# Gate and up of six shared chunks of batches 0 and 1 made jointly, in seven block products

## What is computed

```python
# layer 0: mixture of experts; each expert and the shared one is a gated MLP, 256 -> 1024 -> 256
mlp = lambda x, g, u, d: (gelu(x @ g) * (x @ u)) @ d
x = x + mlp(x, shared) + sum(w[b, e] * mlp(x, skill[e]) for the top 2 experts e of softmax(cond_8[b]))
# layer 1: one expert (argmax of cond_8[b]), 256 -> 512 -> 256, with biases
x = x + (silu(x @ Wu.T + bu) * (x @ Wg.T + bg)) @ Wd.T + bd
# layer 2: x + x @ (sum_g cond_8[b, g] * weight[g] * mask).T + bias
# layer 3: x + x @ W_base.T + b_base + 2 * sum_e cond_8[b, e] * (x @ A[e].T) @ B[e].T
```

## Time and profile before

| | |
|---|---|
| median of 3 runs | 483.42 us (483.36 to 483.56) |
| span of the profiled execution, from its first to its last instruction | 481.8 us |
| its own time | not in the page; 1.6 us lie between its span and the runs' median |
| granted TensorE clock | 1.00 of full speed in all 40 slices |
| TensorE matmul | busy 477.8 us (99%), 2184 matmuls |
| TensorE weight load | 398.5 us (83%) |
| VectorE | 374.9 us (78%) |
| ScalarE | 262.7 us (55%) |
| DMA | 48.9 MB, mean 101 GB/s |

### The profile page before, as it was taken

How to read it: one execution, slowest core, us unless ns; L and a number is a source line. 1 busy time by engine, 2 the same in 40 slices (tenths; PEclk the granted TensorE clock), 3 DMA queues, 4 the chain that set the end, 5 groups by cost and what they waited for, 6 DMA issues and landing times.

```text
span 481.8 us, 6729 instructions
## 1 busy us (share of the span) xinstructions
PE 477.8 (99%) x2184; PEld 398.5 (83%) x2184; DVE 374.9 (78%) x642; ACT 262.7 (55%) x418; POOL 33.7 (7%) x56
## 2 busy tenths in 40 slices
PE   9999999999999999999999999999999999999997
PEld 7888888888888888888888888888888888888886
DVE  7678989969536578985988988998887799965465
ACT  5556555545446344555547566676765365544432
POOL 1910302000100200000000020000000100000000
PEclk9999999999999999999999999999999999999999
DMA  7988985386230532424290053404059224000002
GB/s 224 199 184 201 261 168 153 71 195 134 70 106 0 136 106 67 131 67 131 78 180 4 2 149 93 131 1 131 0 117 205 74 66 128 4 1 0 2 0 87
DMA packets 114538, 48.90 MB, mean 101 GB/s; under 512 B 66552, under 2 KB 113272, under 8 KB 114504
## 3 DMA queue, kind: packets, MB, share of 16 engines
q1 hardware_dynamic: 111360, 42.88, 35.9%
q0 software_dynamic: 2560, 5.21, 4.5%
q10 hardware_dynamic: 584, 0.39, 0.3%
HBM read 46.36 MB, written 2.10 MB: 101 GB/s over the span
## 4 chain that ended last, share of the span: by engine, by line
PE 99%; DVE 0%; DVEq 0%; issue 0%
PE bank_a L1568 9%; PE bank_a L1569 9%; PE bank_b L1569 9%; PE bank_a L1570 9%; PE bank_b L1570 9%; PE bank_b L1568 9%; PE out L1593 6%; PE out L1596 6%; PE out L1592 6%; PE tail L1593 2%; PE tail L1596 2%; PE tail L1592 2%; PE tail L1570 2%; PE tail L1569 2%; PE tail L1568 2%; PE bank_a L1825 2%
## 5 line engine op out<-in xcount | busy, mean ns | idle before, releaser
L706 ACT ACTIVATE hid_hi<-hid 128x512 fp32r<-128x512 f32 x96 | 60.7, 632 | 93.2 <-DVE hid L968 54.0
L976 DVE TENSOR_TENSOR hid_lo<-hid,hid_hi 128x512 fp32r<-128x512 f32 x96 | 66.0, 687 | 16.8 <-ACT hid_hi L706 16.8
L698 ACT ACTIVATE hid<-bank_a 128x512 f32<-128x512 f32 x80 | 47.7, 596 | 55.1 <-PE bank_a L1570 54.3
L968 DVE SCALAR_TENSOR_TENSOR hid<-bank_b,mine,hid 128x512 f32<-128x512 f32 x64 | 47.7, 746 | 32.8 <-PE bank_b L1570 30.6
L956 DVE TENSOR_TENSOR w_lo<-raw,w_hi 128x768 fp32r<-128x768 f32 x57 | 54.1, 949 | 0.4 <-ACT w_hi L665 0.4
L1568 PE MATMUL bank_a<-x_hi,w_hi 128*128 128x512 f32 x114 | 44.5, 391 | 0.0
L1569 PE MATMUL bank_a<-x_lo,w_hi 128*128 128x512 f32 x114 | 44.5, 390 | 0.0
L1570 PE MATMUL bank_a<-x_hi,w_lo 128*128 128x512 f32 x114 | 44.4, 390 | 0.0
L1570 PE MATMUL bank_b<-x_hi,w_lo 128*128 128x512 f32 x114 | 44.4, 389 | 0.0
L1569 PE MATMUL bank_b<-x_lo,w_hi 128*128 128x512 f32 x114 | 44.4, 389 | 0.0
L1568 PE MATMUL bank_b<-x_hi,w_hi 128*128 128x512 f32 x114 | 44.4, 389 | 0.0
(11 more groups left out here) (346 smaller groups left out, 1108.9 us busy)
## 6 DMA issues: line engine op xcount, KB each, us to landing
raw<-in_L_cond_skill_gate SPq DMA_DIRECT2D x32, 256.0 KB, 3.0
raw<-in_L_cond_skill_up SPq DMA_DIRECT2D x32, 256.0 KB, 3.2
raw<-in_L_cond_skill_down SPq DMA_DIRECT2D x64, 128.0 KB, 3.3
raw<-in_L_cond_shared_down SPq DMA_DIRECT2D x22, 128.0 KB, 3.8
raw<-in_L_cond_shared_gate SPq DMA_DIRECT2D x10, 256.0 KB, 3.6
raw<-in_L_cond_shared_up SPq DMA_DIRECT2D x10, 256.0 KB, 3.7
raw_gate<-in_L_cond_W_gate SPq DMA_DIRECT2D x16, 128.0 KB, 3.0
early<-in_L_cond_weight POOLq DMA_DIRECT2D x2, 1024.0 KB, 7.6
```

The lines of the kernel that those rows point to most:

```text
L698: nc.scalar.activation(hid[:, tile_of(g)], bank_a[tile_of(g)][:, :], func, **kw).then_inc(act_ready, 1)
L706: nc.scalar.activation(hid_hi[:, tile_of(g)], hid[:, tile_of(g)], ACT.Copy).then_inc(hid_hi_ready, 1)
L968: ins = nc.vector.scalar_tensor_tensor(tile, bank, weight, tile, ALU.mult, ALU.mult)
L976: nc.vector.tensor_tensor(hid_lo[:, tile], hid[:, tile], hid_hi[:, tile].bitcast(F32), ALU.subtract).then_inc(hid_lo_ready, 1)
```

## The change

Batch 0 now has 2 shared chunks of its own (0, 1) and 16 expert chunks; batch 1 likewise. The other 6 shared chunks are made in 6 units for both, interleaved with chunks 12 to 17 of batch 0. So batch 0 is `first_head` (12 chunks) and 6 units, batch 1 is `second` (18 chunks with layers 1 to 3 of batch 0). The second pair keeps its 8 units. `pair_unit` and what it calls get the pair's first batch as an argument.

Constants (those that matter):

```diff
-MINE_AT = 3
-X_TURN_AT = {4: 1, 7: 2, 9: 3}
-L3_TURN_AT = 6
-L1_AFTER = 5
-C_AT = 13
-CA_AT = CH - 1
+PAIRED = {0: 0, 2: 6}
+JOINT = 2
+SHARED = 2
+OWN = (SHARED + 2 * MLP_CHUNKS, SHARED + 2 * MLP_CHUNKS, 2 * MLP_CHUNKS, 2 * MLP_CHUNKS)
+L1_PLACE = {1: 4, 2: 3, 3: OWN[3]}
+MINE_AT = 1
+X1_TURN_AT, X1_HI_AT, X1_LO_AT = 3, 4, 4
+W2_AT = 8
+T_AT = {5: 0, 7: 1, 9: 2, 10: 3}
+T_HI_AT = {8: ((0, 2), (2, 3)), 9: ((1, 4), (3, 5))}
+MAIN_AT = 10
+SUMS_AT = {0: 10, 2: 4}
+SUMS_LO_AT = {0: 11, 2: 5}
+C_PLACE = {0: 9, 1: 11, 2: 1, 3: 3}
+CA_PLACE = {6: 0, 14: 1}
+PAIR_TURN = {0: {1: 0, 2: 1, 3: 2, 4: 3}, 2: {1: 0, 2: 1, 4: 2, 6: 3}}
+PAIR_TURN_AT = {0: {2: 0, 3: 1, 4: 2, 5: 3}, 2: {2: 0, 3: 1, 5: 2, 7: 3}}
+PIECE_ORDER = ([("own", 0, c) for c in range(0, 14, 2)] + [("joint", 0, 2), ("own", 0, 14), ("joint", 0, 4), ("own", 0, 16), ("joint", 0, 6)]
+               + [("own", 1, c) for c in range(0, OWN[1], 2)]
```

SyncE's order. Piece 0 holds the two shared chunks of batch 0; every later piece is in the loop:

```diff
-            load_piece(1, None, *shared)
-            load_piece(2, None, *shared)
-            load_piece(3, splits_done(0, 1), *shared)
-            load_x(1)
             sp.wait_ge(chosen_ready, 1)
-            expert_pieces(0, 0, {1: lambda: load_x(2), 2: lambda: load_x(3)})
+            for j, (kind, b, c) in enumerate(PIECE_ORDER):
+                if j == 0:
+                    continue
...
+                load_piece(j, *(rows if kind == "own" and own_skill >= 0 else shared))
+                if (kind, b, c) == ("own", 0, 4):
+                    load_x(1)
+                if (kind, b, c) == ("own", 0, 14):
+                    for n in range(3):
+                        first_l1(n)
+                if (kind, b, c) == ("own", 1, 2):
+                    sp.wait_ge(turn_f, 3 * C1)
+                    load_x(2)
+                    load_x(3)
```

GpSimd's queue:

```diff
-            pool.wait_ge(x_turn, B - 1)
+            pool.wait_ge(x_turn, 1)
+            pool.wait_ge(split_lo, splits_done(0, W2_AT))
```

VectorE, at the start and in the new head of batch 0 (ScalarE casts the main weights of unit 0 in chunk `MAIN_AT`):

```diff
             first_parts(0)
+            take_chosen()
             first_x_parts(0)
...
+            take_picks()
+            first_head()
+            for m in range(UNITS[0]):
+                pair_unit(0, m)
+            second()
...
+            def first_head():
+                for i in range(UNIT_AT[0]):
...
+                    if i + SPLIT_AHEAD <= UNIT_AT[0]:
+                        split(0, i + SPLIT_AHEAD)
+                    if i:
+                        hidden_lo(0, i)
...
+                    if i in T_AT:
+                        first_combined(T_AT[i])
+                    if i == C_PLACE[0]:
+                        c3_sum(0)
+                    if i == SUMS_AT[0]:
+                        pair_sums(0, 0)
+                    if i == MAIN_AT + 1:
+                        pair_main_lo(0, 0)
+                    if i == SUMS_LO_AT[0]:
+                        pair_sums_lo(0, 0)
```

TensorE:

```diff
-            batch(0, False)
-            batch(1, True)
+            first_head()
+            for m in range(UNITS[0]):
+                pair_unit(0, m)
+            second()
...
+            def first_head():
+                for i in range(UNIT_AT[0]):
+                    l0_gate_up(0, i)
+                    if i:
+                        l0_down(0, i - 1)
+                    if i == C_PLACE[0]:
+                        c_product(0)
...
                 if m:
-                    pair_down_of(m - 1, 1)
-                else:
-                    ca_product(PAIR)
+                    pair_down_of(b, m - 1, 1)
+                elif b == JOINT:
+                    ca_product(b)
...
             def c_product(b):
...
-                elif b < PAIR:
+                elif b < JOINT:
                     pe.wait_ge(out_ready, 2 * b)
-                elif b > PAIR:
+                else:
                     pe.wait_ge(xs_ready, 4 * (b - 1) + 2)
```

More of the change, by code:

```diff
@@ L554, in later_skill @@
[L554 to L565 removed]
+            sp.wait_ge(chosen_ready, 1)
@@ L655, in split @@
             def split(b, i):
-                if b >= PAIR:
-                    return later_split(b, i)
-                p = i // 2
-                act.wait_ge(raw_in[raw_slot(p)], 64 * raw_uses(b, p))
-                if i - W_SLOTS >= 2:
-                    wait(act, down_done, hiddens_before(b) + hidden_of(b, i - W_SLOTS) + 1)
-                elif not first(b):
-                    last = max(c for c in range(CH) if c >= 2 and (c - i) % W_SLOTS == 0)
-                    act.wait_ge(down_done, hiddens_before(b) - CH + last + 1)
@@ new lines, in pair_unit @@
+                if not last:
+                    pair_main_hi(b, m + 1)
+                else:
+                    split(b + 1, 0)
+                if (b, m) == (JOINT, 1):
+                    weights_split_hi(ca_hi, tail[:, 1, :], (tail_ready, tails_before(JOINT) + product_of(JOINT, "ca")))
+                act.wait_ge(pair_product, PRODUCTS * unit + 3)
+                wait(act, pair_hid_lo, 2 * unit)
+                if (b, m) == (JOINT, 0):
+                    act.wait_ge(xs_lo_ready, 4 * JOINT)
@@ new lines, in pair_unit @@
+                nc.scalar.activation(low_sum, bank_x[b][:, :], ACT.Copy).then_inc(pair_copy, 1)
+                activate(b, n, ACT.Gelu_apprx_tanh)
+                act.wait_ge(pair_product, PRODUCTS * unit + 4)
+                nc.scalar.activation(high_sum, bank_y[b][:, :], ACT.Copy).then_inc(pair_copy, 1)
+                if not last:
+                    pair_sums_hi(b, m + 1)
+                    split(b, own + 1)
+                else:
+                    split(b + 1, 1)
+                if m in PAIR_TURN_AT[b]:
+                    turn_chunk_hi(b, PAIR_TURN_AT[b][m])
@@ L1270, in batch, with second @@
+            def second():
+                b = 1
+                for i in range(OWN[b]):
                     n = hidden_of(b, i)
-                    if i == MLP_CHUNKS:
+                    if i == 0:
+                        pair_hidden_lo(0, UNITS[0] - 1, 0)
+                        pair_hidden_lo(0, UNITS[0] - 1, 1)
+                    if i == SHARED:
                         dve.wait_ge(mine_staged, b + 1)
-                    m = i // MLP_CHUNKS
-                    hidden(b, n, weight=mine[:, m - 1:m] if m else None)
@@ L1439, in pair_head @@
+                hidden_lo(b, n)
             def pair_head():
-                b = PAIR
-                for i in range(MLP_CHUNKS):
+                b = JOINT
+                for i in range(UNIT_AT[b]):
                     n = hidden_of(b, i)
@@ L1823, in pair_product_of @@
+                v_hi, v_lo = (cols(x, *n) if isinstance(n, tuple) else combined(b0, x, n) for x in (x_hi, x_lo))
                 w, w2 = w_hi_blocks[:, start + block], w_lo_blocks[:, start + block]
@@ L1941, in _ @@
             route()
-            batch(0, False)
-            batch(1, True)
+            first_head()
+            for m in range(UNITS[0]):
+                pair_unit(0, m)
+            second()
             pair_head()
-            for m in range(MLP_CHUNKS):
-                pair_unit(m)
+            for m in range(UNITS[JOINT]):
+                pair_unit(JOINT, m)
             pair_rest()
```

1114 lines of the change are left out of this document (567 added, 547 removed).

## The result

The changed kernel takes 500.12 us (median of 4 runs, 498.74 to 503.47); the kernel before took 483.49 beside it (4 runs, 483.36 to 483.69). The ratio is 1.0341, interval 1.0297 to 1.0385: 16.6 us slower, where 483.3 with a range up to 485.0 was forecast. The profiled execution has a span of 499.2 us and a time of its own of 500.9.

A forecast was written before the change was run, and what follows sets the result against it. TensorE's instruction stream was taken as the bound: 18 removed matmuls (-4.08 us) against four new waits (+1.35, +1.8, +0.55, +0.3) sum to -0.08 us on 483.42, forecasting 483.3 us, range 482.0 to 485.0.

The forecast's parts named there:

- The removed matmuls: Shared chunks of batches 0 and 1: 18 matmuls go, at 0.2267 us each, -4.08 us.
- Start: Chunk 2 of batch 0: first expert piece waits for routing, lands at 12.7; TensorE +1.35 us later (0.85 to 2.6).
- Nothing follows piece 1 within 2 us: Start of batch 0: argument against the first expert piece landing late, given with that rival.
- The rival with a late piece: Start: first expert piece takes 5.7 us to land rather than 3.1; start costs 3.95, result 485.9 us; chance 0.18.
- Entry of unit 0: First unit: TensorE waits for VectorE's main-weight subtraction behind chunk 11's hidden_lo; +1.8 us (1.6 to 2.2).
- unit 0 to unit 1: Nothing replaces ca_product between the units, so TensorE waits for Gelu's bank and hidden_lo; +0.55 us (0.3 to 0.8).
- The weights of unit 2: In unit 1: shared chunks 4 and 5 wait for own chunk 13's split, delaying ScalarE's low-sum copy; +0.3 us (0 to 0.7).
- the pieces behind them are wanted later than they land: SyncE's queue: pieces behind the moved loads of x 2 and 3 come in time; listed as costing nothing.
- In `second` VectorE has 84 of 96 us: Batch 1: VectorE's load fits; worst place 1.8 us late with ca_product (1.4 us) beside it; listed as costing nothing.
- the sum: Whole kernel: -4.08 + 1.35 + 1.8 + 0.55 + 0.3 = -0.08 us, giving 483.3 us.
- A new wait in `second`: Batch 1: sign that would make the prediction wrong on the slow side; no size given.
- The clock at its full level through both gaps: Expected sign: clock stays full through the gaps at chunk 2 (about 1.4 us) and unit 0 (about 1.8 us).

The follow-up runs named there:

- l1b: Changed kernel with batch 0's layer-1 load groups behind own (0,12), own (0,14) and joint (0,4), the third thus behind the joint piece; 493.72 us.
- l1: Changed kernel with batch 0's three layer-1 load groups behind own (0,12), joint (0,2), own (0,14) rather than all behind own (0,14); 495.55 us.
- quietfull: `place` with GpSimd's queue reordered: bias tensors and their row's round trip first, layer 2's weights behind; 485.51 us, ratio 1.0032.
- place: `all`, but layer 2's weights and bias tensors loaded from chunk 11, and the second layer-1 group behind joint (0,2); 486.97 us.
- three: Changed kernel with `bias` and `l1` edits, and main weights of unit 0 cast in chunk 9 instead of 10; 488.73 us.
- all: Changed kernel with `bias`, `l1b` and `w2late` edits together, and main weights of unit 0 cast in chunk 9; 493.71 us.
- w2late: Changed kernel with GpSimd's loads of layer 2's weights and bias tensors moved from chunks 8 and 11 of batch 0 to chunk 15; 503.26 us.
- bias: Changed kernel with bias steps of layers 2 and 3 moved from chunks 6, 7, 8 of batch 1 to 0, 1, 3; 492.11 us.
- stalls: Kernel before, with TensorE held up at four chunks of batch 3 by chains of 3, 5, 7 and 9 GpSimd memsets; 501.89 us.
- quiet: `quietfull` with the first expert piece of batch 0 in two halves, chunk 2's first; 485.32 us.
- warm: `place` with the first expert piece in two halves and six filling matmuls ahead of TensorE's wait for the routing; 487.33 us.

## Why the prediction was wrong

**The removed matmuls: right.** 2166 matmuls, and every account above closes with 4.08 us.

**Start: mechanism right, size wrong.** SyncE's first expert issue stands at 7.95 (7.85 foretold). The term of +1.35 was mis-sized: the last DMA landed 4.9 us after its issue rather than 3.1, the gap was 2.71, and 1.8 us, most of it low clock, came on top: 4.52. "Nothing follows piece 1 within 2 us" does not hold either. The last DMA of piece 1 starts at about 9.8, and the next piece right behind it:

```profile
10.49 0.46 SPq L480 DMA_DIRECT2D raw<-in_L_cond_skill_gate  x1
```

Whether that made the landing slow was not tried. The gap is no constant: with the same code at the start and no low clock near 7 us it was 1.42 (`l1b`), 1.50 (`l1`), 2.24 (`quietfull`), 2.30 (`place`), 2.48 (`three`), 2.55 (`all`) and 2.71. The rival with a late piece is near: by its own working a landing of 4.9 makes 3.1 us. It missed the clock.

**Entry of unit 0 and unit 0 to unit 1: right.** +1.8 foretold, 2.00 of gap and 2.27 lost; +0.55 foretold, 0.54 lost. For unit 0 the steps are there one by one: hidden at 59.12, hidden_lo 1.44 us later (60.56), pair_main_lo 0.61 behind it.

**The weights of unit 2: the first failed step.** The prediction wrote "the piece with shared chunks 4 and 5 waits for the split of own chunk 13" and gave it +0.3, and of SyncE's queue it said "the pieces behind them are wanted later than they land". The piece did not wait for the split but for the twelve layer-1 DMAs put directly ahead of it. I had followed x, the pieces and layer 2's weights through the queue, and not this group, which the diff moves; that one such group can hold the queue for 8.65 us was to be read in the trace of before. The path behind the landing (cast, copy of the low sum, bank) was right. The cast began at 79.66 instead of 75.3 (slot free at 70.6, 1.5 of issue, 3.2 to land): 2.9 us of this is the queue (first issue at 73.43), 1.5 the piece's own slower issue and landing. It cost 5.83 us. `l1b`, which only changes who stands first, takes it away; `w2late`, which only empties the other queue, takes most of it away. Both are causes: the order, and the traffic that stretched the issue. That traffic was moved by the change as well: BIAS_LOADS_AT went from 18 to 11, a constant that the list under "The change" leaves out, and the bias tensors with it from 76 us, behind the layer-1 loads, to 52. The prediction speaks of layer 2's weights alone.

**Batch 1: the second failed step, and the largest.** "In `second` VectorE has 84 of 96 us" counts VectorE's load and no round trips. BIAS_AT moved from 3 to 8 (also left out of that list), and nowhere did I put that beside `output` in chunk 10 and c_product in chunk 11; the term is missing from the sum, which is to say that it stood at nothing. The trip of 16 us was to be read in the trace of before. It cost 7.90 us, and `bias` gives 8.0 back. "A new wait in `second`" did stand among the signs of being wrong on the slow side, without a price.

**"The clock at its full level through both gaps": wrong.** The stretches I argued from had no gaps in them. It fell behind three of the four waits: 1.8 + 1.8 + 2.4 = 6.0 us, which no rival held. By `stalls` about 0.3 of each is the restart, so some 5.2 are the clock.

Together: the spans differ by +17.4 us where the sum said -0.08. Of these 17.5 us, 7.9 are batch 1, 5.5 unit 1, 3.2 the start beyond its term, 0.5 the entry of unit 0 and 0.4 elsewhere. Nor was the gain there once the schedule was mended: the best of 15 versions that compute the same (`quiet`, 485.32 us) is 1.7 us slower than the kernel before beside it (483.64), and by their medians none beat it. Whether another placing of the bulk would is open. The largest wait that is left in `quietfull` is the start's (2.5 us).

## What to carry to other kernels

When a diff moves a step, follow it on every queue to its last reader: a group of loads delays what stands behind it by its issue time under load, and a value that makes a round trip through HBM needs its full trip (17 us here) between writer and reader. An idle TensorE costs more than its gap: behind nearly all gaps of 2.5 us and more seen here, 1.3 to 2.8 us of low clock came on top. Moving bulk transfers away from one deadline puts them on another, so lay them out against all deadlines at once, small broadcasts too.

## Not expected of the hardware

- The granted clock fell behind single gaps of 2.5 us, with TensorE busy up to the gap, and in two executions behind 2.0. In six of the 17 profiles of the changed kernel and its versions, matmuls stood 0.43 us apart near 7 us, at the very first chunk, with hardly a gap before it; the six extra fillings of `warm` did not narrow the spread, and this stays open.
- The changed kernel and its versions spread by 2 to 7 us where most runs of the kernel before lie within 0.7. In `place` the time goes with the granted clock: four runs at 0.992 and 0.993 took 488.7 to 489.8 us, three at 1.00 took 484.0 to 485.8. In `warm` it does so only in part (483.6 to 487.1 at 1.00), so something else adds to it.
- Issue time is no constant: four DMAs of 128 KB of layer 1 took 2.9 us with nothing of GpSimd's queue beside them, 6.4 beside the bias tensors, 7.5 beside row u and 13.64 beside layer 2's 2 MB and the bias tensors.
- Beside a broadcast load of 64 KB the last two of four DMAs of weights took a median of 5.4 us to land instead of 3.1; beside the bias tensors those of the first joint piece took 8.1 instead of 3.0.
